# A two-layer attention and mixture kernel on one core: the eight experts of layer 0 get only the tokens routed to them, in 15 blocks of 128 slots

## The chip, the core and the metric

One core of a Trainium2 chip runs the whole program. The metric is device time in microseconds of that core; lower is better. Five engines work side by side, each in its own program order: TensorE (PE), VectorE (DVE), ScalarE (ACT), GpSimd (POOL), and SyncE (SP), which here only issues transfers. They meet through semaphores.

## What is computed

The input is 8 sequences (called batches below) of 512 tokens with 128 numbers each. Layer 0 adds a latent attention (16 heads of 8) and a mixture of experts to the input. Layer 1 adds a mix of three attentions and a gated feed-forward of width 512. The part that the change touches is the mixture:

```
logits = jnp.einsum('bsd,de->bse', x, Wg) + bg
_, top_idx = jax.lax.top_k(logits, K)          # K = 2 of E = 8
sel = jnp.sum(jax.nn.one_hot(top_idx, E, dtype=logits.dtype), axis=-2) > 0
masked = jnp.where(sel, logits, -jnp.inf)
gates = jax.nn.softmax(masked, axis=-1)
for e in range(E):
    h = jax.nn.relu(jnp.einsum('bsd,dh->bsh', x, W1[e]) + b1[e])     # 128 -> 512
    y = jnp.einsum('bsh,hd->bsd', h, W2[e]) + b2[e]                  # 512 -> 128
    out = out + gates[..., e:e + 1] * y
```

Each token has two experts with a gate above zero. The two four-head attentions of layer 1, called `ca` and `mc` here, are the other part: `softmax(q k) v` with 512 keys per sequence.

## The kernel before

**Time grid.** A table `AT` gives every piece of work of a batch a step number G, and each engine walks through the steps in order and does what is due in it. Batch b is shifted by `S = 80` steps, so that in steady state three batches overlap and every 80 steps the pattern repeats. Work at step 112 of one batch stands beside step 32 of the next; below, "step" is the number modulo 80, from 0 to 79, and a "cycle" is 80 such steps. Each step holds one attention unit (two heads of one chunk of 128 queries): PE makes two score tiles, DVE takes their row maxima (L725 for the causal groups `a0`, L729 for the others), 15 steps later PE makes the transposed scores, ACT takes the exponentials into `probs`, and every second step PE multiplies by the values. Steps 0 to 31 hold the units of `a0`, 32 to 39 `ca`, 40 to 63 and 72 to 79 `a1`, 64 to 71 `mc`. PE may not write a score tile before DVE has reduced the tile two before it (semaphore `max`), so PE and DVE stay within about a step of each other. No engine passes by a waiting instruction.

**Experts.** `up(b, i)` (32 per batch, steps 7 to 40) makes 128 of an expert's hidden rows for all 512 tokens: three float16 passes (high and low halves of weights and tokens) of 512 columns into bank U. ACT reads the bank twice, for `hm` (L1060) and `h_hi` (L1061), and POOL subtracts for `h_lo` (L1162). `down(b, e, c)` (32 per batch, steps 15 to 45) is 12 matmuls of 128 columns into bank N. DVE adds each expert's output times its gate to `xs` (L829, 4 per expert, steps 17 to 45). All experts run on all tokens; the gates of the others are zero. All weights lie in SBUF as `w_hi` and `w_lo` from the start.

**Gates.** `rank_parts` compares all pairs of logits (L764 to L775, steps 78 and 79), and `gate_weights` follows at step 6.

**Key sums.** In `ca` and `mc`, `value(g, c)` multiplies the exponentials of chunk c with the values (4 float32 matmuls, `probs,vc`) and then with ones (4 more, `probs,ones`) for the softmax denominators: four chunks for each of the 16 groups.

**Feed-forward and others.** `fa`, `fb`, `glu`, `g1`, `g2`, `f3` of the batch before run at steps 51 to 79 and 0 to 11; DVE scales each of their banks (L882, L887, L892), POOL makes low halves (`glu_low`, L1203). POOL also sums the rotary parts (L1182 and `halves`, steps 50 and 65), masks the causal tiles (L1150) and takes square roots (L1169). SP issues the transfers that spread q and k over partitions (`relq`, `relk`) and the row maxima (`mrow`).

## Time and profile before

| | us |
|---|---|
| median of three runs | 1853.18 (1851.37 to 1859.51) |
| the profiled execution | 1848.13 |
| its span, first to last instruction | 1846.4 |
| PE busy in the span | 1654.0 (90%) |
| DVE / ACT / POOL busy | 1206.7 / 1171.5 / 690.3 |
| data moved by transfers | 66.82 MB |

The page of the profile has the busy times, 40 slices of the span, the transfer queues, the chain of work that ended last, the groups of instructions and the transfers. A busy PE time is a union of instructions whose ends include the drain of the array; the distance between two starts tells what a matmul costs in a stream. The stages of a cycle are read by windows of time: the pairs of DVE's row maxima were counted, two per step, to find where the steps of batch 4 begin.

### The profile page before, as it was taken

What the parts mean: (1) busy time and instruction counts of PE and PEld (TensorE: products, weight loads), DVE (VectorE), ACT (ScalarE), POOL (GpSimd) and SP (SyncE); (2) the same over time, 40 slices, a digit from 0 to 9 for tenths busy, and PEclk for the clock granted to TensorE, in tenths of its full rate; (3) what the DMA queues carried; (4) which work ended last, traced back from release to release, by engine and by line L of the source; (5) the groups of instructions that cost most, each with busy time, mean ns of one, the idle gap of its engine ahead of it and who ended that gap; (6) DMA issues with size and microseconds to landing.
All of it is one profiled execution on the core that took longest, in us unless ns stands there. A gap on an engine that the chain in (4) does not pass through costs nothing.

```text
span 1846.4 us, 33580 instructions
## 1 busy us (share of the span) xinstructions
PE 1654.0 (90%) x12402; PEld 707.3 (38%) x12402; DVE 1206.7 (65%) x3101; ACT 1171.5 (63%) x2226; POOL 690.3 (37%) x672
## 2 busy tenths in 40 slices
PE   3886899889999999999999999999999999988876
PEld 1343453245333543345333543345333543322231
DVE  6545478556876588666876588666876568476633
ACT  2681766577656875687657865687666865635442
POOL 3453652255232652255232652255232641211120
PEclk9996999999999999999999999999999999989986
DMA  5101100101101101101101101101100100010010
GB/s 212 35 19 35 59 19 16 55 13 30 47 23 36 42 25 41 47 19 30 47 24 36 42 24 46 41 18 31 45 30 31 36 24 24 31 39 18 18 35 6
DMA packets 63683, 66.82 MB, mean 36 GB/s; under 512 B 8144, under 2 KB 58144, under 8 KB 62624
## 3 DMA queue, kind: packets, MB, share of 16 engines
q1 hardware_dynamic: 63520, 64.68, 11.4%
q8 instruction: 99, 1.62, 0.4%
q14 instruction: 64, 0.52, 0.1%
HBM read 40.73 MB, written 23.59 MB: 35 GB/s over the span
## 4 chain that ended last, share of the span: by engine, by line
PE 71%; DVE 12%; ACT 10%; issue 5%; DMA 1%; POOL 1%; SPq 1%; POOLq 0%; ACTq 0%; DVEq 0%
PE banks L366 69%; DVE negmax L729 5%; ACT probs L1000 3%; ACT h_hi L1061 2%; DVE h L892 2%; ACT hm L1060 2%; ACT L1000 1%; DVE r_b L917 1%; ACT h L1095 1%; DVE h L887 1%; PE banks L586 1%; DVE xs L829 1%; ACT L1095 0%; DVE g_t L882 0%; DVE mrow L736 0%
## 5 line engine op out<-in xcount | busy, mean ns | idle before, releaser
L1000 ACT ACTIVATE probs<-banks 128x512 f32<-128x512 f32 (+3 forms) x1280 | 614.3, 535 | 442.8 <-PE banks L366 438.6
L729 DVE TENSOR_REDUCE negmax<-banks 128x1 f16<-128x512 f32 x768 | 493.0, 685 | 149.7 <-PE banks L366 146.6
L1162 POOL TENSOR_TENSOR h_lo<-hm,h_hi 128x512 f16<-128x512 f32 x256 | 296.6, 1159 | 383.2 <-ACT h_hi L1061 383.1
L725 DVE CUSTOM_DVE_ANT_0 scr<-banks,mask_row 128x384 f32<-128x384 f32 (+3 forms) x512 | 230.3, 487 | 212.0 <-PE banks L366 210.2
L366 PE MATMUL banks<-kp,qs 32*128 32x512 f16 (+3 forms) x1024 | 236.0, 361 | 46.6 <-DMA kp<-relk 22.4
L1060 ACT ACTIVATE hm<-banks,cols 128x512 f32<-128x512 f32 x256 | 177.3, 693 | 105.7 <-PE banks L366 104.5
L366 PE MATMUL banks<-probs,vp 128*32 128x512 f32 (+3 forms) x2048 | 241.8, 545 | 0.0
L366 PE MATMUL banks<-qs,kp 32*128 32x512 f16 (+3 forms) x1024 | 199.5, 355 | 35.6 <-ACT probs L1000 32.6
L1203 POOL TENSOR_TENSOR h_lo<-h,h_hi 128x512 f16<-128x512 f32 x96 | 110.3, 1169 | 290.1 <-ACT h_hi L1089 212.4
L366 PE MATMUL banks<-w_hi,h_hi 128*128 128x128 f16 x1152 | 204.0, 220 | 0.0
L366 PE MATMUL banks<-w_lo,h_hi 128*128 128x128 f16 x1152 | 203.6, 220 | 0.0
L366 PE MATMUL banks<-w_hi,h_lo 128*128 128x128 f16 x1152 | 203.5, 220 | 0.0
L366 PE MATMUL banks<-qkc 97*128 97x512 f16 (+1 forms) x512 | 166.6, 400 | 12.2 <-DMA qkc<-mrow 4.3
L1061 ACT ACTIVATE h_hi<-banks,cols 128x512 f16<-128x512 f32 x256 | 176.2, 688 | 0.0
L366 PE MATMUL banks<-xh,w_hi 128*128 128x512 f16 x320 | 127.5, 399 | 49.4 <-ACT h_hi L1061 30.7
L366 PEld LDWEIGHTS banks<-kp,qs 32*128 32x128 f16 x1024 | 63.4, 92 | 264.8 <-issue 101.8
L366 PE MATMUL banks<-xl,w_hi 128*128 128x512 f16 x320 | 124.4, 389 | 0.0
L366 PEld LDWEIGHTS banks<-w_hi,h_hi 128*128 128x128 f16 x1152 | 113.2, 98 | 29.2 <-issue 11.7
L366 PE MATMUL banks<-xh,w_lo 128*128 128x512 f16 x320 | 124.3, 389 | 0.0
L366 PEld LDWEIGHTS banks<-w_lo,h_hi 128*128 128x128 f16 x1152 | 113.2, 98 | 18.1 <-issue 0.7
L366 PEld LDWEIGHTS banks<-w_hi,h_lo 128*128 128x128 f16 x1152 | 113.2, 98 | 0.0
L1154 POOL TENSOR_TENSOR halves<-w,halves 128x512 f16<-128x512 f32 x64 | 74.5, 1164 | 98.5 <-ACT halves L1020 96.6
(163 smaller groups left out, 2377.2 us busy)
## 6 DMA issues: line engine op xcount, KB each, us to landing
qkc<-relm SPq DMA_DIRECT2D x96, 128.0 KB, 2.9
qs<-relq SPq DMA_DIRECT2D x64, 128.0 KB, 2.1
kp<-relk SPq DMA_DIRECT2D x64, 128.0 KB, 2.2
relm<-halves SPq DMA_DIRECT2D x32, 256.0 KB, 2.1
relq<-halves SPq DMA_DIRECT2D x16, 256.0 KB, 2.1
relk<-halves SPq DMA_DIRECT2D x16, 256.0 KB, 2.1
h<-split_in SPq DMA_DIRECT2D x3, 1024.0 KB, 5.2
xs<-x_in SPq DMA_DIRECT2D x8, 256.0 KB, 2.8
```

The lines of the kernel that those rows point to most:

```text
L366: return nc.tensor.matmul(psum[rows_, bank, cols_], lhsT, rhs, start=start, stop=stop)
L586: last = nc.tensor.transpose(psum[:, M, ch(c)], osb[:, g.main % 2, ch(c)], C("ident"))
L725: v.tensor_tensor_reduce(scr[:, s, 0:kw], psum[:, SCO + s, 0:kw], mask_row[:, T - kw:T], -1.0, 3e38, ALU.add, ALU.min, negmax[:, g.n % 2, ...
L729: v.tensor_reduce(negmax[:, g.n % 2, c, h:h + 1], psum[:, SCO + s, 0:kw], AX.X, ALU.max, negate=True).then_inc(sem("max"), 1)
L829: ins = v.scalar_tensor_tensor(out=xs[:, b % 4, c, :], in0=psum[:, N, ch(c)], scalar=gates[:, c, e:e + 1], in1=xs[:, b % 4, c, :], op0=ALU ...
L892: v.tensor_scalar(h32[:, o, :], psum[:, U, :], V(f"hs{n}", o), None, ALU.mult) \
L1000: a.activation(probs[:, c % 2, 2 * pair + s, q0:T], psum[:, TRA + s, q0:T], ACT.Exp, scale=SCALE[main(g)]).then_inc(sem("exp"), 1)
L1060: a.activation(hm[:, i % 2, :], psum[:, U, :], ACT.Relu, bias=V("b1", i))
L1061: a.activation(h_hi[:, (e + 1) % 2, hc, :], psum[:, U, :], ACT.Relu, bias=V("b1", i)) \
L1154: p_.tensor_tensor(out=halves[:, w, 1, :], in0=w32[:, w, :], in1=halves[:, w, 0, :], op=ALU.subtract).then_inc(sem(f"low{w}"), 1)
L1162: p_.tensor_tensor(out=h_lo[:, (e + 1) % 2, hc, :], in0=hm[:, i % 2, :], in1=h_hi[:, (e + 1) % 2, hc, :], op=ALU.subtract).then_inc(sem("h ...
L1203: p_.tensor_tensor(out=h_lo[:, k % 2, o, :], in0=h32[:, o, :], in1=h_hi[:, k % 2, o, :], op=ALU.subtract).then_inc(sem("g_lo"), 1)
```

## The change

- **Routing.** `rank_parts` moves from steps 78 and 79 to 45, 46 and 47 of the same cycle, the one before the batch's own, and `gate_weights` from step 6 of its own cycle to 51 of the one before. PE then counts, for every token and expert, the chosen tokens before it (`positions`, 8 small matmuls, step 51), and DVE turns the counts into two slot numbers per token and into the owner expert of each of `NT = 15` blocks of 128 slots (`slots`, 14 operations, step 52; `pick`, 5 operations, step 53). A block belongs to one expert. 1024 routed tokens in blocks of one expert never need more than 15 blocks, and all 15 are always computed.
- **Scatter and gather.** ACT and POOL make high and low halves of the normalised tokens (`xr`), and POOL issues 8 indirect transfers that write them to slots in HBM (`xslots`, steps 53 to 56). SP loads the slots back (`xg_load`), PE turns them (8 transposes per four blocks), ACT copies them out. After the experts, ACT copies the block outputs (`y_out`), SP stores them (`yslots`), POOL issues 8 indirect transfers that gather each token's two rows (steps 44 to 50), and DVE adds them with their gates (8 operations, step 53).
- **Experts.** `up(b, t)` is 12 matmuls of 128 columns for a block (every second step from 10 to 38), ACT makes `hm` in 4 operations of 128 columns, DVE copies its high half (`hh`), POOL makes the low half (`hl`), and `down(b, t)` is 12 matmuls of 128 columns (every second step from 13 to 41).
- **Weights.** At the start the split expert weights are written to HBM (`wexp1`, `wexp2`, 4 MB). For each block SP reads the owner from SBUF into a register, twice, and loads 264 KB and 256 KB (`wup`, `wdn`; 30 loads per batch, three buffers each).
- **Key sums.** In `ca` and `mc` POOL adds the exponentials of chunks 1 and 2 into those of chunk 0 (`psums`, 4 additions of 1024 numbers per partition, steps 50 to 53 and 2 to 5), and PE multiplies `probs` (chunk 3) and `psums` with ones at the last chunk only. ACT waits for the addition before it writes over `probs`.
- Some other pieces move by one or two steps. `scr` becomes bfloat16, and several buffers share space.

```diff
-AT.update({("up", i): at for i, at in enumerate((
...
+AT.update({("up", t): 10 + 2 * t for t in range(NT)})
+AT.update({("down", t): 13 + 2 * t for t in range(NT)})
+AT.update({("wup", t): 6 + 2 * t for t in range(NT)})
+AT.update({("wdn", t): 8 + 2 * t for t in range(NT)})
+AT.update({("scatter", c): at for c, at in enumerate((-27, -26, -25, -24), 0)})
+AT.update({("gather", c): at for c, at in enumerate((44, 46, 48, 50), 0)})
+AT.update({("xg_load", q): at for q, at in enumerate((-22, -21, 8, 16), 0)})
...
-                    three(U, slice(0, T), [(part(w_hi, "W1", i, P), part(w_lo, "W1", i, P), xh[:, 0, :], xl[:, 0, :])]) \
...
+                def up(b, t):
...
+                    pe.wait_ge(sem(f"wup{n % 3}"), 16 * (n // 3 + 1))
+                    own("u", ("up", t), b)
+                    w = wt1[:, n % 3, 0:512].bitcast(F16)
+                    for hc in range(HC):
+                        last = three(U, ch(hc), [(w[:, P * hc:P * hc + P], w[:, 512 + P * hc:512 + P * hc + P],
+                                                  xt[:, q % 2, t % 4, 0, :], xt[:, q % 2, t % 4, 1, :])])
...
-                    if not main(g):
-                        last.then_inc(sem("pv_mix"), 1)
-                        for h in range(GH):
-                            last = mm(N, slice(q0, T), ones[:, :], probs[:, c % 2, h, q0:T], c == 0, c == NC - 1,
-                                      rows_=slice(32 * h, 32 * h + 32))
                     last.then_inc(sem("pv"), 1)
+                    if not main(g) and c == NC - 1:
+                        pe.wait_ge(sem("psums"), 4 * (g.mix + 1))
+                        own("n", "den", g.n)
+                        for part_ in (keys(g, c), psums):
+                            for h in range(GH):
+                                last = mm(N, slice(0, T), ones[:, :], part_[:, h, :], part_ is not psums, part_ is psums,
...
+                            v.tensor_copy(hh[:, n % 2, :], hm[:, n % 2, :]).then_inc(sem("hh"), 1)
+                    if (b := due(G, "add")) is not None:
+                        dve.wait_ge(sem("gath"), 128 * (b + 1))
...
-                            a.activation(hm[:, i % 2, :], psum[:, U, :], ACT.Relu, bias=V("b1", i))
-                            a.activation(h_hi[:, (e + 1) % 2, hc, :], psum[:, U, :], ACT.Relu, bias=V("b1", i)) \
+                            for hc in range(HC):
+                                ins = a.activation(hm[:, n % 2, ch(hc)], psum[:, U, ch(hc)], ACT.Relu, bias=bias[:, hc:hc + 1])
...
+                            for k in range(2):
+                                p_.indirect_dma_start(xslots, bass.IndirectOffsetOnAxis(idx[:, NC * k + c:NC * k + c + 1], 0),
+                                                      xr[:, c, :, :].rearrange("p a d -> p (a d)"), None).then_inc(sem("scat"), 16)
...
+                                p_.indirect_dma_start(yg[:, NC * k + c, :], None, yslots,
+                                                      bass.IndirectOffsetOnAxis(idx[:, NC * k + c:NC * k + c + 1], 0)).then_inc(sem("gath"), 16)
...
+                    p_.tensor_tensor(out=psums[:, hs, :], in0=psums[:, hs, :], in1=probs[:, c % 2, hs, :],
+                                     op=ALU.add).then_inc(sem("psums"), 1)
...
+                    e = sp.value_load(owner[0:1, t:t + 1], min_val=0, max_val=E - 1)
+                    sp.dma_start(wt1[:, n % 3, :], wexp1[bass.ds(e, 1), :, :].rearrange("e p f -> (e p) f")).then_inc(sem(f"wup{n % 3}"), 16)
```

On PE, in the expert stage of a middle batch (`xh`, `xl` tokens, `w_hi`, `w_lo` weights, `kp,qs` and `qs,kp` attention tiles), the kernel before has this:

```order
L366 MATMUL banks<-kp,qs 128x512 x2
L366 MATMUL banks<-qs,kp 128x512 x2
L366 MATMUL banks<-probs,vp 32x512 x4
L366 MATMUL banks<-xh,w_hi 128x512
L366 MATMUL banks<-xl,w_hi 128x512
L366 MATMUL banks<-xh,w_lo 128x512
L366 MATMUL banks<-oc,wide 128x512
L366 MATMUL banks<-kp,qs 128x512 x2
L366 MATMUL banks<-qs,kp 128x512 x2
L366 MATMUL banks<-xh,w_hi 128x512
L366 MATMUL banks<-xl,w_hi 128x512
L366 MATMUL banks<-xh,w_lo 128x512
```

And the changed kernel, at the same place (`xt` turned tokens, `wt` loaded weights, `xg` slots):

```order
L434 MATMUL banks<-kp,qs 128x512 x2
L434 MATMUL banks<-qs,kp 128x512 x2
L434 MATMUL banks<-probs,vp 32x512 x4
L434 MATMUL banks<-xt,wt 128x128 x12
L434 MATMUL banks<-oc,wide 128x512
L434 MATMUL banks<-kp,qs 128x512 x2
L434 MATMUL banks<-qs,kp 128x512 x2
L635 MATMUL banks<-ident,xg 128x128 x8
```

Three matmuls of 512 columns in every step have become twelve of 128 in every second one, with the transposes of slots between.

On DVE, at steps 51 to 54 of a middle batch, the kernel before has row maxima, the heads of layer 0 and the gated feed-forward:

```order
L729 TENSOR_REDUCE negmax<-banks 128x1 x4
L842 RECIPROCAL rden<-banks 128x4x4
L843 TENSOR_TENSOR onorm<-banks,rden 128x4x32
L729 TENSOR_REDUCE negmax<-banks 128x1 x2
L882 SCALAR_TENSOR_TENSOR g_t<-g_t,banks 128x512
L729 TENSOR_REDUCE negmax<-banks 128x1 x2
```

The changed kernel has this between the end of the same heads (step 52) and the same feed-forward operation (step 54):

```order
L898 TENSOR_TENSOR first<-first,off 128x32
L899 TENSOR_TENSOR first<-first,off 128x32
L900 TENSOR_TENSOR late_f<-const,till 1x128
L902 TENSOR_REDUCE best<-first 128x4
L903 TENSOR_REDUCE best<-first 128x4
L906 CAST idx<-best 128x8
L907 TENSOR_REDUCE cnt<-late_f 1x16
L910 TENSOR_SCALAR owner<-cnt 1x16
L825 TENSOR_REDUCE negmax<-banks 128x1 x2
L984 SCALAR_TENSOR_TENSOR xs<-yg,gk,xs 128x128 x8
L915 TENSOR_TENSOR first<-first,best 128x32 x2
L919 TENSOR_TENSOR first<-first,gates 128x32 x2
```

Six more operations of `slots` stand ahead of these and one of `pick` behind. So 14 new operations stand in step 52 and 13 in step 53, with only one pair of row maxima between them.

On POOL, at steps 49 to 57 of a middle batch, before:

```order
L1154 TENSOR_TENSOR halves<-w,halves 128x512 x2
L1182 TENSOR_TENSOR w<-r_a,r_b 128x512
L1184 CAST halves<-w 128x512
L1154 TENSOR_TENSOR halves<-w,halves 128x512
L1203 TENSOR_TENSOR h_lo<-h,h_hi 128x512 x3
L1221 TENSOR_TENSOR oc<-oc,r_b 128x512
```

And in the changed kernel (`psums` are the key sums, the DMA rows the indirect transfers):

```order
L1379 TENSOR_TENSOR psums<-psums,probs 128x1024
L1368 DMA yg<-yslots,idx 128x128 x2
L1398 TENSOR_TENSOR w<-r_a,r_b 128x512
L1400 CAST halves<-w 128x512
L1335 TENSOR_TENSOR halves<-w,halves 128x512
L1379 TENSOR_TENSOR psums<-psums,probs 128x1024 x3
L1353 DMA xslots<-xr,idx 1920x256 x8
L1419 TENSOR_TENSOR h_lo<-h,h_hi 128x512 x3
L1437 TENSOR_TENSOR oc<-oc,r_b 128x512
```

Four additions and ten transfers now stand around the rotary sum and ahead of the feed-forward's low halves.

## Rows read from the trace of the kernel before

**Rows 1.** The page: span, and busy time of each engine.

```profile
span 1846.4 us, 33580 instructions
PE 1654.0 (90%) x12402; PEld 707.3 (38%) x12402; DVE 1206.7 (65%) x3101; ACT 1171.5 (63%) x2226; POOL 690.3 (37%) x672
```

**Rows 2.** The page: chain that ended last, share by engine.

```profile
PE 71%; DVE 12%; ACT 10%; issue 5%; DMA 1%; POOL 1%; SPq 1%; POOLq 0%; ACTq 0%; DVEq 0%
```

**Rows 3.** Windows, batch 4: steps 0-6, 7-31, 32-45, 46-63, 64-79; busy by engine.

```profile
771.05:789.81 18.76, 18.73 (x123) 6.47 (x122) 9.32 (x37) 11.50 (x21) 1.13 (x1) 1.00 0.06 21
789.81:852.82 63.01, 58.90 (x591) 31.70 (x591) 38.30 (x138) 51.87 (x102) 38.41 (x37) 1.00 0.12 31
852.82:887.69 34.87, 34.28 (x349) 18.80 (x348) 28.23 (x74) 24.61 (x59) 19.07 (x20) 1.00 0.07 17
887.69:934.56 46.87, 43.78 (x262) 15.53 (x260) 38.39 (x75) 27.95 (x53) 11.91 (x11) 0.96 0.14 43
934.56:978.62 44.06, 41.25 (x236) 13.99 (x236) 32.71 (x65) 28.08 (x47) 14.41 (x15) 0.96 0.15 49
```

**Rows 4.** Timeline of PE: start, us, form; an `up`, then 24 matmuls of `down`.

```profile
642.45 0.39 PE L366 MATMUL banks<-xh,w_hi 128*128 128x512 f16 x1
...
643.11 0.22 PE L366 MATMUL banks<-w_hi,h_hi 128*128 128x128 f16 x1
...
644.39 0.22 PE L366 MATMUL banks<-w_hi,h_lo 128*128 128x128 f16 x1
```

**Rows 5.** Timeline of PE: a key sum and what follows it.

```profile
700.97 1.04 PE L366 MATMUL banks<-probs,ones 128*32 128x512 f32 x8
701.94 0.39 PE L366 MATMUL banks<-xh,w_hi 128*128 128x512 f16 x1
```

**Rows 6.** Groups of instructions with shapes apart: count, busy us, mean ns, idle before.

```profile
L366 PE MATMUL banks<-probs,ones 128*32 128x512 f32 x512 | 70.4, 623 | 0.0
...
L1060 ACT ACTIVATE hm<-banks,cols 128x512 f32<-128x512 f32 x256 | 177.3, 693 | 105.7 <-PE banks L366 104.5
L1061 ACT ACTIVATE h_hi<-banks,cols 128x512 f16<-128x512 f32 x256 | 176.2, 688 | 0.0
L1000 ACT ACTIVATE probs<-banks 128x128 f32<-128x128 f32 x128 | 28.5, 280 | 29.9 <-PE banks L366 29.9
```

**Rows 7.** The same of DVE: additions of experts, high halves, a two-input operation.

```profile
L829 DVE SCALAR_TENSOR_TENSOR xs<-banks,gates,xs 128x128 f32<-128x128 f32 x256 | 71.8, 343 | 29.4 <-PE banks L366 29.4
...
L900 DVE CAST h_hi<-h 128x512 f16<-128x512 f32 x64 | 28.2, 494 | 0.0
...
L770 DVE TENSOR_TENSOR r_a<-r_a,r_b 128x256 f32<-128x256 f32 x8 | 8.4, 1052 | 0.3
```

**Rows 8.** Timeline of DVE: rank operations at 163 to 167 us.

```profile
165.38 0.43 DVE L770 TENSOR_TENSOR r_a<-r_a,r_b 128x256 f32<-128x256 f32 x1
...
166.38 0.18 DVE L774 TENSOR_REDUCE gmax<-lg 128x4 f32<-128x32 f32 x1
166.60 0.19 DVE L775 TENSOR_TENSOR lg<-lg,gmax 128x32 f32<-128x32 f32 x1
```

**Rows 9.** The same of POOL: low halves.

```profile
L1162 POOL TENSOR_TENSOR h_lo<-hm,h_hi 128x512 f16<-128x512 f32 x256 | 296.6, 1159 | 383.2 <-ACT h_hi L1061 383.1
```

**Rows 10.** Timeline of all engines in the first 40 us.

```profile
20.19 1.27 POOL L1182 TENSOR_TENSOR w<-r_a,r_b 128x512 f32<-128x512 f32 x1 [4.68 <-DVE r_b L756]
...
25.93 5.55 DVE L982 TENSOR_TENSOR w_lo<-probs,w_hi 128x2048 f16<-128x2048 f32 x2
26.09 3.24 POOL L1182 TENSOR_TENSOR w<-r_a,r_b 128x512 f32<-128x512 f32 x1 [2.72 <-DVE r_b L756]
...
38.01 0.43 SPq L1272 DMA_DIRECT2D kp<-relk  x1
38.36 0.29 PE L366 MATMUL banks<-kp,qs 32*128 32x128 f16 x2 [13.07 <-DMA kp<-relk]
```

**Rows 11.** Window: batch 0 from its first steps to the end of its experts.

```profile
43.00:148.00 105.00, 88.97 (x783) 45.23 (x783) 54.54 (x191) 72.42 (x147) 51.28 (x51) 1.00 0.08 24
```

**Rows 12.** The page: transfers; KB each, median us from issue to landing.

```profile
xs<-x_in SPq DMA_DIRECT2D x8, 256.0 KB, 2.8
```

More of the change, by code:

```diff
@@ L170, in first_time @@
 def first_time(name, b):
-    return min(time((*name, c), b) for c in range(NC)) if name[0] == "down" else time(name, b)
+    return time(("down", 4 * name[1]), b) if name[0] == "y" else time(name, b)
 def numbered(names, more=()):
@@ L238, in build @@
         LOWS[name, b] = lows[w]
+    OLD, last = {}, {}
+    for g in GROUPS:
+        for c in range(NC):
+            k = c % 2 if main_kind(g.kind) or c else 2
+            OLD[g.n, c] = last.get(k)
+            last[k] = (g, c)
     CAUSAL = {g.n: n for n, g in enumerate(g for g in GROUPS if g.kind == "a0")}
@@ L458, in value @@
                             taken(pe, "m", "cav" if g.kind == "ca" else "mcv", g.b)
-                            own("n", "den", g.n)
                     _, q0 = width(g, c)
```

478 lines of the change are left out of this document (356 added, 122 removed), and 8 rows, old and new, of the table AT.

## The prediction

> **What bounds the kernel now.** I read the page's busy times first, then the chain, then windows of one cycle in the middle. PE is busy 1654.0 of 1846.4 us [rows 1], and 71% of the chain that ended last runs through it [rows 2]. The average hides that the stages of a cycle differ [rows 3]. In steps 7 to 31 PE is busy 58.9 of 63.0 us, with ACT behind it at 51.9. In steps 32 to 45 it is 34.3 of 34.9, with DVE at 28.2. In steps 46 to 63 PE has 43.8 of 46.9 and DVE already 38.4. In steps 64 to 79 it is 41.3 and 32.7 of 44.1. So PE sets the pace everywhere, but in the last two stages DVE follows closely. PE can't leave DVE behind by more than a step, because of the row maxima. What matters is therefore which engine is busiest in each stage after the change.
>
> **Part 1, expert matmuls.** The three passes of an `up` take 643.11 - 642.45 = 0.66 us; 24 matmuls of 128 columns have 1.28 us from the first start to the last, 0.056 each, so twelve take 0.67 [rows 4]. Before: 32 x 0.66 + 32 x 0.67 = 42.6 us per batch. After: 15 ups and 15 downs of twelve, 20.1, and 30 transposes of 128 columns at 0.056, 1.7, and 8 small matmuls, at most 0.4: 22.2. PE saves 20.4 us per batch. (15 blocks are always computed, so the work falls to about half, not to 2 in 8.)
>
> **Part 2, key sums.** One chunk's sum costs 701.94 - 700.97 = 0.97 us [rows 5]; 512 matmuls in the group, 8 to a chunk, are 8 chunks per batch [rows 6]. Four stay: 3.9 us saved. On PE alone that is (20.4 + 3.9) x 8 = 194 us, a span of 1652. That is the floor, not the forecast.
>
> **Part 3, the stages one by one.** Steady cycle, starting from the windows [rows 3].
> - Steps 7 to 31. PE loses 23 ups and 19 downs (27.9), gets 11 ups and 10 downs (14.1), transposes (1.7) and one key sum more (1.0): 58.9 becomes 47.8. ACT loses 23 pairs of readings at 0.69 each, 31.7, and gets 44 operations of 128 columns at 0.28 (12.3) and copies of about 7 at 0.69 per 512 columns [rows 6]: 39. DVE loses 16 additions of 0.343 and gets 11 copies of 0.49 [rows 7]: 38. POOL loses 23 low halves of 1.16 and gets 11 [rows 9]. PE still leads. With the gap of before, 4.1, the window is 52: -11.0.
> - Steps 32 to 45. PE loses 9 ups and 13 downs (14.6) and gets 9 pieces of 0.67: 25.7. DVE: 28.2 - 5.5 + 4 x 0.49 + 0.9 for the first rank operations = 25.6. Two engines that wait for each other at equal load leave more gaps than one: 29.5, -5.4.
> - Steps 0 to 6. Three of four key sums of `mc` leave: -2.6.
> - Steps 46 to 63. Here the change works against itself. DVE gets the rest of the rank work (2.9), gate weights (4 x 0.22), `slots` (14 x 0.22 = 3.1), `pick` (5 x 0.22 = 1.1) and 8 additions at 0.343 (2.7). The 0.22 is the distance of two linked small operations [rows 8]. Sum 10.6, so DVE has 49.0, PE 43.8 - 1.9 + 0.4 = 42.3: DVE is now the bound, and the 27 operations in steps 52 and 53 come as one lump, which PE can't run past. With the gap of before (3.1) the window is 52.1: +5.2.
> - Port waits in that stage. When DVE and POOL both work on SBUF they delay each other: a rotary sum took 1.27 us alone and 3.24 beside two large DVE subtractions [rows 10], and a two-input DVE operation took 0.43 alone [rows 8] and 1.05 on average [rows 7]. POOL is now full in steps 50 to 56: four additions of 1024, at twice 1.16 = 2.3 us each [rows 9], and three rotary pieces. Each can hold up one DVE operation: between 0 and 9.3 + 3.1 = 12.4 us. I take 4, about seven meetings at the 0.6 us that the row shows. Stage in all: +9.2.
> - The Trainium skill ("SBUF — State Buffer", SBUF: two separate sides) calls the port pair that the two share an exclusive lock for a whole instruction, and warns that a POOL-issued transfer can't get its descriptors written while DVE holds it. The slowed rows agree with the lock; by the full rule the stage would carry the whole 12.4 us and the span would be 50 us longer.
> - Steps 64 to 79. The rank work has left; PE is the bound: -1.
>
> Sum over the cycles: seven batches in steady state x (-16.4) = -115; seven times -2.6 = -18; six cycles x (+9.2) = +55, and +1.5 in the seventh; six x (-1) = -6. Together -82.
>
> **Part 4, the start and batch 0.** PE's first score waits for the k transfer until 38.4 us, and that chain runs through a rotary sum on POOL [rows 10]. Ahead of it now stand the rank work and `slots` on DVE (about 5 us) and 8 indirect transfers on POOL: +12. Batch 0 runs its experts with little beside them: 105 us, PE 89.0 [rows 11]. The 20.4 us of PE come off nearly whole: -20. After its last block nothing covers the way back: `y_out` 0.7, store 2.8 [rows 12], 8 gathers, landing 2.8, additions 2.7, less the additions of before: +14. A last key sum or two: -2. Together +4.
>
> **Part 5, transfers and what hides them.** Block loads are 30 x 260 KB per batch, 62 MB more beside 66.8 MB. A transfer of 256 KB lands in 2.8 us [rows 12], and each load is issued four steps ahead, of about 2.1 us each. Hidden. On SP a load needs an issue of 0.43 us [rows 10] and a register read. No row shows the read: between 0.43 (an issue) and 2.8 (a transfer's round trip). Two loads must fit into two steps, 4.2 us, so up to 1.7 us a read is free. I take 1. An indirect transfer on POOL isn't in the trace either: between 0.43 (an issue) and 2.8 (a round trip), below nothing excluded since POOL issued none. I take 1.0, nearest to POOL's own operations of 1.16 [rows 9]. In a steady cycle it is covered: from step 50 POOL has 10 transfers, 9.3 us of additions, 3.1 of rotary pieces and a low half, 24 us, and the first that PE misses is the low half at step 62, 12 steps or 35 us later. The Trainium skill ("DMA: Bandwidth & Descriptors", Anatomy of one DMA — SWDGE (gpsimd) path) gives about 2.0 us fixed for such a transfer, mostly until its completion is confirmed; if POOL were held for it, an estimate from that page is +18 us at the start and at batch 0's end, and the steady cycles would just hold.
>
> **The sum.** 1846.4 - 82 + 4 = 1768 us of span. The profiled run's own time is 1.7 above its span, and the median of the runs shown 5.1 above that: 1775.
>
> **Rivals.**
> - *PE alone counts.* The new DVE work fits into gaps, and the port waits don't come. For it: PE leads in all five windows. Against: 49.0 us of DVE can't fit into 46.9 [rows 3]. 1652 plus the start's 26 gives 1678, as a median 1685. Chance 0.17.
> - *The gain is lost in steps 46 to 63.* Port waits at their upper bound, 8.4 x 6 = +50, and PE's granted clock falling to 1.2 GHz in longer gaps, as it did to a mean of 0.96 in this window: 1825 to 1860. Chance 0.17.
> - *Slower: POOL's indirect transfers.* Ten stand ahead of the low halves. With T us each the free 35 us are used up at T = 2.1; at T = 3.2 the gain of 78 us is gone; at T = 4 it is 19 us per cycle, +133 and the start's longer waits: about 1910. Also behind them: SP at step 58 waits for the scatter and holds back the row maxima of the next group. Chance 0.13.
> - *Slower: SP's register reads.* At 2.8 us a block needs 6.5 us against 4.2: 34 us per batch, about 1970 after the gain. It decides from 2.0 us a read, where 10 us per batch are lost. Chance 0.05.
> - My forecast, 1715 to 1825: chance 0.48.
>
> **How the numbers follow.** The likeliest case gives 1775. Below 1665 nothing reaches but mistakes in the floor; above 1870 lies most of the two slower rivals. The range is 1665 to 1870. A measurement here can tell about 0.5% from no change, 1844 to 1862. Faster: 0.48 + 0.17 + most of the second rival, 0.75. Same: 0.06. Slower: 0.19.
>
> **What would show it.** In the profile after: PE busy near 1480 us; steps 7 to 31 at 50 to 54 us with PE waiting little; steps 46 to 63 at 52 to 57 us, longer than now, with PE waiting for DVE's maxima at the lump and DVE's two-input operations above their lone durations; first score near 50 us. Wrong if PE waits for `wt` loads, if POOL's low halves come late to `g1`, or if the stage 46 to 63 hasn't grown.

## The result: slower by 2.7%

The changed kernel takes 1905.5 us (median of 4 runs, 1898.5 to 1909.1), the kernel before, run beside it, 1854.5 (1851.4 to 1859.5). The ratio is 1.0268, with a 95% interval of 1.0230 to 1.0306. I had forecast 1775 in a range of 1665 to 1870, so the sign is wrong too. Run 5 and v2 below each had one execution in a much slower state (3282 and 2461 us); these are in no median or ratio here, and v2's stages are read from its second run. The page of the changed kernel, lines that answer to [rows 1, 2]:

```profile
span 1904.7 us, 34002 instructions
PE 1548.5 (81%) x11490; PEld 658.2 (35%) x11490; DVE 1290.5 (68%) x3199; ACT 1038.7 (55%) x2258; POOL 812.5 (43%) x728
PEclk9985887999899998999899998999898998979876
PE 52%; DVE 19%; issue 10%; ACT 9%; POOL 4%; DMA 3%; SPq 3%; POOLq 0%; ACTq 0%; DVEq 0%
```

TensorE has 105 us less to do and is idle 164 us more. Its share of the chain that ended last went from 71 to 52%. The five windows of batch 4, as in [rows 3] (steps 0 to 6, 7 to 31, 32 to 45, 46 to 63, 64 to 79; the columns are length, then busy time and number of instructions of each engine, granted clock, DMA share, GB/s):

```profile
804.16:820.81 16.65, 16.62 (x100) 5.75 (x99) 8.65 (x32) 11.04 (x20) 10.41 (x5) 1.00 0.16 48
820.81:882.84 62.03, 52.13 (x584) 29.62 (x584) 38.94 (x132) 42.63 (x112) 26.25 (x26) 0.97 0.51 141
882.84:914.22 31.38, 28.15 (x270) 15.14 (x273) 26.08 (x65) 18.64 (x53) 12.23 (x14) 0.94 0.30 91
914.22:974.20 59.98, 46.40 (x262) 15.63 (x263) 54.41 (x117) 27.13 (x53) 37.14 (x31) 0.84 0.20 60
974.20:1019.33 45.13, 41.31 (x227) 13.57 (x227) 31.00 (x54) 28.22 (x47) 14.40 (x14) 0.92 0.14 45
```

Set against the forecast (us; the last column is version v2, below, in its second run):

| steps | before | forecast | changed | v2 |
|---|---|---|---|---|
| 0 to 6 | 18.8 | 16.2 | 16.7 | 19.2 |
| 7 to 31 | 63.0 | 52.0 | 62.0 | 54.9 |
| 32 to 45 | 34.9 | 29.5 | 31.4 | 30.1 |
| 46 to 63 | 46.9 | 56.1 | 60.0 | 47.6 |
| 64 to 79 | 44.1 | 43.1 | 45.1 | 45.4 |
| cycle | 207.6 | 196.8 | 215.2 | 197.3 |

A cycle is 18.4 us over the forecast, 10.0 of them in steps 7 to 31. The start came as forecast: the first score is at 48.7 us, 10 later than before. Over the whole run, in us against the kernel before: start +10.3, batch 0 (its steps 0 to 79) +1.2, batches 1 and 2 +14.5, batches 3 to 6 +7.6 each, the rest +1.8.

**What stands in the lump.** VectorE's timeline of step 52 (start, us, engine, line, operation, tiles) shows the slot arithmetic:

```profile
932.97 0.17 DVE L897 TENSOR_TENSOR till<-till,begin 128x8 f32<-128x8 f32 x1
933.17 1.15 DVE L898 TENSOR_TENSOR first<-first,off 128x32 f32<-128x32 f32 x1
934.25 0.18 DVE L899 TENSOR_TENSOR first<-first,off 128x32 f32<-128x32 f32 x1
934.46 2.31 DVE L900 TENSOR_TENSOR late_f<-const,till 1x128 f32<-1x128 f32 x1
936.70 0.17 DVE L902 TENSOR_REDUCE best<-first 128x4 f32<-128x32 f32 x1
936.99 2.01 DVE L906 CAST idx<-best 128x8 uint32<-128x8 f32 x1
938.91 0.27 DVE L907 TENSOR_REDUCE cnt<-late_f 1x16 f32<-1x128 f32 x1
939.22 2.08 DVE L910 TENSOR_SCALAR owner<-cnt 1x16 int32<-1x16 f32 x1
```

GpSimd at the same time (the third line is the second of the three additions by itself), and after it TensorE's next score, with what it waited for in brackets:

```profile
933.13 1.15 POOL L1335 TENSOR_TENSOR halves<-w,halves 128x512 f16<-128x512 f32 x1
934.24 7.03 POOL L1379 TENSOR_TENSOR psums<-psums,probs 128x1024 f32<-128x1024 f32 x3
936.59 2.38 POOL L1379 TENSOR_TENSOR psums<-psums,probs 128x1024 f32<-128x1024 f32 x1
941.95 1.20 PE L434 MATMUL banks<-kp,qs 32*128 32x512 f16 x2 [9.78 <-DVE negmax L825]
```

The three additions take 2.33 to 2.39 us and end at 936.63, 938.97 and 941.27. L900, L906 and L910 end at 936.77, 939.00 and 941.30, each just behind one of them, and L898 ends at 934.32, behind L1335 at 934.28. An operation on sixteen numbers took 2.08 us. The reductions between them took 0.16 to 0.27, and L899, which starts 0.01 us after the first addition, took 0.18. GpSimd's additions weren't stretched by it (their mean over the run is 2.362).

**What TensorE waited for in all** (total us, times, longest); in the trace of before the first of these groups had 12.6 us in 45 waits:

```profile
PE banks L434 <- DVE negmax L825: 86.0, 79, 9.9
PE banks L434 <- ACT probs L1165: 50.3, 39, 3.0
PE banks L434 <- issue: 39.8, 35, 5.8
```

### The profile page after: what moved, and what is told of

It reads as the page before. It is cut to its first block, busy times and chain, and to the rows that moved or that the text cites. A ratio compares the mean times of both kernels' runs of the same rounds, so it can differ in the third digit from the quotient of the medians.

```text
span 1904.7 us, 34002 instructions
## 1 busy us (share of the span) xinstructions
PE 1548.5 (81%) x11490; PEld 658.2 (35%) x11490; DVE 1290.5 (68%) x3199; ACT 1038.7 (55%) x2258; POOL 812.5 (43%) x728
## 4 chain that ended last, share of the span: by engine, by line
PE 52%; DVE 19%; issue 10%; ACT 9%; POOL 4%; DMA 3%; SPq 3%; POOLq 0%; ACTq 0%; DVEq 0%
PE banks L434 50%; DVE negmax L825 7%; ACT probs L1165 3%; ACT hm L1234 3%; DVE h L1049 1%; DMA qkc<-relm 1%; SPq L1509 1%; DVE pack L832 1%; DVE r_b L1074 1%; ACT L1165 1%; POOL xslots L1353 1%; DVE xs L984 1%; DVE xn L846 1%; POOL yg L1368 1%; ACT h L1276 1%
## 5 line engine op out<-in xcount | busy, mean ns | idle before, releaser
L821 DVE CUSTOM_DVE_ANT_0 scr<-banks,mask_row 128x384 bf16<-128x384 f32 (+3 forms) x512 | 230.1, 487 | 166.7 <-PE banks L434 164.9
L1359 POOL TENSOR_TENSOR hl<-hm,hh 128x512 f16<-128x512 f32 x120 | 139.0, 1158 | 260.3 <-DVE hh L979 260.2
L1379 POOL TENSOR_TENSOR psums<-psums,probs 128x1024 f32<-128x1024 f32 x64 | 149.7, 2362 | 128.1 <-PE banks L434 128.1
L1234 ACT ACTIVATE hm<-banks,wt 128x128 f32<-128x128 f32 x480 | 137.6, 370 | 116.7 <-PE banks L434 116.1
L434 PE MATMUL banks<-wt,hh 128*128 128x128 f16 x960 | 96.3, 223 | 34.3 <-issue 29.4
L434 PE MATMUL banks<-xt,wt 128*128 128x128 f16 x1440 | 107.0, 227 | 6.0 <-issue 5.8
L434 PE MATMUL banks<-h_hi,w_hi 128*128 128x512 f16 x256 | 98.9, 386 | 9.6 <-DVE h L1049 8.8
L434 PEld LDWEIGHTS banks<-xt,wt 128*128 128x128 f16 x1440 | 86.6, 102 | 52.6 <-issue 48.6
L1335 POOL TENSOR_TENSOR halves<-w,halves 128x512 f16<-128x512 f32 x64 | 74.1, 1158 | 57.4 <-ACT halves L1185 55.1
L434 PE MATMUL banks<-h_hi,w_lo 128*128 128x512 f16 x256 | 97.8, 382 | 0.0
L434 PE MATMUL banks<-h_lo,w_hi 128*128 128x512 f16 x256 | 97.7, 382 | 0.0
```

Of the source, the lines that this page charges most:

```text
L434: return nc.tensor.matmul(psum[rows_, bank, cols_], lhsT, rhs, start=start, stop=stop)
L821: v.tensor_tensor_reduce(scr[:, s, 0:kw], psum[:, SCO + s, 0:kw], mask_row[:, T - kw:T], -1.0, 3e38, ALU.add, ALU.min, negmax[:, g.n % 2, ...
L1234: ins = a.activation(hm[:, n % 2, ch(hc)], psum[:, U, ch(hc)], ACT.Relu, bias=bias[:, hc:hc + 1])
L1335: p_.tensor_tensor(out=halves[:, w, 1, :], in0=w32[:, w, :], in1=halves[:, w, 0, :], op=ALU.subtract).then_inc(sem(f"low{w}"), 1)
L1359: p_.tensor_tensor(out=hl[:, n % 2, :], in0=hm[:, n % 2, :], in1=hh[:, n % 2, :], op=ALU.subtract).then_inc(sem("h_lo"), 1)
L1379: p_.tensor_tensor(out=psums[:, hs, :], in0=psums[:, hs, :], in1=probs[:, c % 2, hs, :], op=ALU.add).then_inc(sem("psums"), 1)
```

## The experiments

Each time is a median; the ratio is to the kernel before, run beside it on the same chip; the changed kernel itself stands at 1.0268 (1.0230 to 1.0306). "Theory A" is the lump behind GpSimd's additions.

**1. Additions made small.**

```
-  out=psums[:, hs, :], in0=psums[:, hs, :], in1=probs[:, c % 2, hs, :]
+  out=psums[:, hs, 0:1], in0=psums[:, hs, 0:1], in1=probs[:, c % 2, hs, 0:1]
```

> The changed kernel, except that each of GpSimd's 64 key sum additions takes one column of 512 per head and so leaves the sums incomplete; every wait and every other instruction stays. Theory A (the lump of slot arithmetic on VectorE in step 52 is slow because each of several of its small operations stands behind a whole 2.3 us addition of GpSimd): step 52 falls from 11.8 us to about 4, the operations at L900, L906 and L910 from 1.6 to 1.8 us to about 0.2, PE's wait of 9.8 us before the next score is nearly gone, and with the clock that is kept the run takes 65 to 90 us less than the changed kernel's 1905: 1815 to 1840. Theory B (these operations are slow by themselves: one partition, conversions to integers): they stay at 1.5 us and more, step 52 stays above 9 us, and the time stays within 20 us of 1905. Theory C (TensorE's lower clock is a cause of its own and not a result of its gaps): the gap goes, the mean granted clock stays near 0.90 and at most half of the gain comes.

Measured 1858.6 us, 1.0044 (1.0019 to 1.0069): 2.2% or 41 us less than the changed kernel. The same operations on VectorE, at the same place:

```profile
924.73 0.28 DVE L900 TENSOR_TENSOR late_f<-const,till 1x128 f32<-1x128 f32 x1
925.23 0.17 DVE L906 CAST idx<-best 128x8 uint32<-128x8 f32 x1
925.61 0.16 DVE L910 TENSOR_SCALAR owner<-cnt 1x16 int32<-1x16 f32 x1
```

Their own cost is 0.16 to 0.28 us and the whole arithmetic takes 2.7 us, so theory B falls. TensorE's wait before the next score is 2.4 us, and step 52 falls from 11.8 to 4.4 us. Steps 46 to 63 are at 55.8 us in the mean of batches 3 to 6, against 60.8 in the changed kernel and 45.7 before. Theory A is right, but for 41 us, not 65 to 90: the additions account for 5.0 of that stage's growth of 15.1 us. Part of what step 52 gives is lost one step earlier, where a small operation of the gate weights (0.19 us in the changed kernel) now meets a rotary sum of GpSimd and ends just behind it:

```profile
920.03 1.39 DVE L928 TENSOR_TENSOR gates<-gates,gsum 128x32 f32<-128x32 f32 x1
920.08 1.28 POOL L1398 TENSOR_TENSOR w<-r_a,r_b 128x512 f32<-128x512 f32 x1
```

Where the stage grew can be read step by step (means of batches 3 to 6, changed kernel less before): steps 46 and 47, where the rank work now stands, 3.0 us, step 52 9.0, step 53 with the additions to `xs` and `pick` 3.2. The signs of theory C came too: the granted clock is 0.90 to 0.91 over the run and 0.86 in this stage (0.84 in the changed kernel), though TensorE's wait shrank from 9.8 to 2.4 us, and about half of the expected gain came. So this run shows what the additions cost, but not whether the lower clock is only a result of the gap.

**2. The key sums alone.** The kernel before, with `value`, `exp_unit` and the new `sum_keys` as in the changed kernel; to make room, small tensors share storage and `scr` is bfloat16, as there.

> The kernel before with only the key sums moved to GpSimd as in the changed kernel (its dense experts stay). To make room, small tensors share storage and the masked scores' scratch is bf16, as in the changed kernel. TensorE has 3.9 us per batch less. Theory A (the additions hurt only because the slot arithmetic meets them): few VectorE operations of the kind that stand behind them are in steps 50 to 53, so the time is 1820 to 1850, 5 to 30 us under before. Rival (GpSimd's additions hold up VectorE's casts and sums, and ScalarE's buffers, wherever they stand): 1860 to 1890, with VectorE's negated maxima coming late in steps 50 to 53 and 2 to 5.

Measured 1848.5 us, 0.9982 (0.9957 to 1.0008). Part 2 by itself is worth nothing or next to it. Steps 46 to 63 stay at 45.9 us, so the additions don't lengthen it there, with two key sums (1.9 us by [rows 5]) taken off TensorE; but steps 7 to 31 go from 63.9 to 67.1 (means of batches 3 to 6), and that takes back the 2.6 us of steps 0 to 6. The price of the additions in the changed kernel comes from meeting the slot arithmetic.

**3. The slot arithmetic 17 steps later, gate weights, `pick` and scatters 17 to 20, the additions left where they are.**

```
-"gates": -29, "pos": -29, "slots": -28, "pick": -27, ... scatter (-27, -26, -25, -24), xg_load (-22, -21, ...)
+"gates":  -9, "pos": -11, "slots": -11, "pick": -10, ... scatter (-10, -9, -8, -7),    xg_load (-3, -2, ...)
```

In this kernel `pick` ran one step ahead of the gate weights, so the picked values weren't the final weights; all instructions are there.

> The changed kernel with the positions, slot arithmetic, gate weights, pick and scatters moved 18 steps later (positions and slots from steps 51 and 52 to 69, gate weights to 71, pick to 70, scatters to 70 to 73, the first slot loads to 77 and 78), where GpSimd does no additions and VectorE has room; the work is all there. Theory A: step 52 falls to about 3.5 us, the lump of some 4 us in steps 69 to 71 mostly fits beside TensorE's work (VectorE was busy 6.5 of 10.7 us there), and the run is 50 to 80 us under the changed kernel: 1825 to 1855; the start is also up to 8 us shorter, since 8 scatters no longer stand ahead of the k transfer. Theory B (the operations are slow by themselves): the lump of 10 us moves along, steps 69 to 71 get 5 us or more longer, and the time is 1890 to 1915.

Measured 1953.4 us, 1.0548 (1.0505 to 1.0592): 50 us slower than the changed kernel, where theory A in my reading wanted it 50 to 80 faster. Steps 64 to 79 grow from 45.4 to 56.0 us, steps 46 to 63 shrink only from 60.8 to 59.5 (means of batches 3 to 6). The by-form groups of VectorE (busy, mean ns), and TensorE and GpSimd at steps 71 and 72:

```profile
L984 DVE SCALAR_TENSOR_TENSOR xs<-yg,gk,xs 128x128 f32<-128x128 f32 x64 | 65.9, 1089 | 9.4 <-DMA yg<-yslots,idx 9.1
L900 DVE TENSOR_TENSOR late_f<-const,till 1x128 f32<-1x128 f32 x8 | 2.2, 280 | 0.3
1014.86 1.08 POOL L1353 DMA_INDIRECT xslots<-xr,idx  x1 [12.27 <-DVE idx L906]
1021.31 0.96 POOL L1353 DMA_INDIRECT xslots<-xr,idx  x1 [0.30 <-issue]
1022.29 1.16 POOL L1391 TENSOR_TENSOR xl<-wide,xh 128x512 f16<-128x512 f32 x1
1023.51 0.61 PE L434 MATMUL banks<-xh,l_hi 128*128 128x512 f16 x1 [6.52 <-POOL xl L1391]
```

Two things. The slot arithmetic is cheap once no addition is beside it (0.28). But the eight additions to `xs`, next in the queue, now stand behind GpSimd's key sums in its place (mean 1089 ns, 421 in the changed kernel), and step 53 takes 11.8 us as step 52 did. And the six scatters seen there, 0.96 us of GpSimd each and 0.30 between two, hold back the low half `xl` that TensorE needs. My fear of transfers on GpSimd was a real mechanism; it was harmless only where the change had put them.

**4. No register reads.** `e = t // 2` in place of both `value_load`, so each block gets a fixed expert's weights.

> The changed kernel with every block's weights loaded from a fixed expert (block number divided by two) instead of the one read from the owner table; sizes, number and waits of the transfers stay, and the results are those of the wrong experts. This takes the 30 register reads a batch off SyncE's queue. My forecast's term (reads of up to 1.7 us are free): within 5 us of 1905. Rival (loads and the transfers queued behind them come late because of the reads, which the trace puts at about 0.8 us each, and cause part of TensorE's waits in steps 7 to 45): 1875 to 1895, with the wait for the qkc transfer at step 31 (1.2 to 1.5 us) gone.

Measured 1909.7 us, 1.0306 (1.0254 to 1.0358): no gain. The reads are free, as forecast.

**5. Downs one step later.**

```
-("down", t): 13 + 2 * t;  y_out (20, 28, 36, 42);  y_store (21, 29, 37, 43);  "ca_spread": 110
+("down", t): 14 + 2 * t;  y_out (21, 29, 37, 42);  y_store (22, 30, 38, 43);  "ca_spread": 109
```

> The changed kernel with each block's second matmul one step later (14 + 2t in place of 13 + 2t), the copies of the first three result banks one step later too, and the mixing transfer of step 30 back at 29 as before the change. Theory D (the gain of steps 7 to 31 went into TensorE's waits for hand-offs: a down that opens a new bank waits for ScalarE's copy y_out, which stands behind four ReLU pieces of the same step, and the first down for POOL's low half; measured gaps of 0.9 to 1.8 us at steps 13, 21, 29, 31 and 37): about 5 to 6 us per batch come back, steps 7 to 45 fall from 93 to 88, the run to 1855 to 1875. Theory E (ScalarE, VectorE and GpSimd are paced by the four-step chain itself, and a wait removed turns up at the next step): within 10 us of 1905.

Measured 1974.7 us, 1.067 (1.061 to 1.073), 69 us slower than the changed kernel. TensorE's waits just ahead of the downs did go (in steps 7 to 45 of batch 4 from 4.1 us in four waits to none over 0.15), but a down and the up two blocks on now stand in the same even step, and the odd steps have neither; the waits for row maxima grew from 86.0 to 102.6 and those of the masked groups from 15.1 to 37.5 us. From step 14 to 41 the even steps take 45.4 us in all in place of 33.9, the odd ones 24.0 in place of 28.9 (means of batches 3 to 6). So how evenly TensorE's work lies over the steps counts, which no busy time shows.

**6. TensorE kept busy through the gap.** `back0`'s four transposes 17 times.

> The changed kernel, in which TensorE repeats the four transposes of back0 (step 53) 17 times over in batches 0 to 6, the same result into the same bank, about 9 us of work in place of the 10 us in which it waited there for VectorE's lump. Theory C (the lower clock that follows the gap is a cost of its own): the granted clock in steps 54 to 63 stays at 1.0, where the trace of the changed kernel counts 4 to 6 us per batch of matmul time added by the half clock in steps 46 to 63, and the run is 15 to 35 us shorter: 1870 to 1890. Rival (those steps are set by VectorE, busy 40.6 of 44.7 us, and the clock only uses up slack): within 8 us of 1905, or longer by what the repeats overrun.

Measured 1910.3 us, 1.031 (1.0265 to 1.0356): no gain. The clock of steps 46 to 63 rose only from 0.84 to 0.86 in batch 4, and the repeats made the stage longer (63.0 us against 60.8, means of batches 3 to 6), so this doesn't decide what the clock costs; it stays open.

**7. One ReLU per block.** The biases of three of the four chunks are left out.

```
-for hc in range(HC): a.activation(hm[:, n % 2, ch(hc)], ..., bias=bias[:, hc:hc + 1])
+a.activation(hm[:, n % 2, :], psum[:, U, :], ACT.Relu, bias=bias[:, 0:1])
```

> The changed kernel with one ReLU of 512 columns per block in place of four of 128 (1.15 us by the trace of the changed kernel, against 0.69 for one of 512 before the change). All four chunks of hidden units get the first chunk's bias, so the other biases are left out. ScalarE loses 15 x 0.46 = 7 us per batch, and the bank that up, xg and ReLU share comes free 0.46 us earlier. Theory D (hand-offs pace steps 7 to 45): 3 to 6 us per batch less, 1865 to 1885. My forecast (TensorE's own work paces them, ScalarE has room at 61 of 93 us): within 8 us of 1905.

Measured 1884.7 us, 1.0165 (1.0116 to 1.0215): 20 us less. ScalarE, with 61 us of work in the 93 of steps 7 to 45, is far from full, and still 7 us per batch taken off it bring something: steps 7 to 31 fall by 2.3 us in the mean of batches 3 to 6. But steps 32 to 63 give 3.2 us back there, at a lower granted clock (0.89 for 0.96 in steps 32 to 45, 0.81 for 0.84 in 46 to 63), and these cycles are 0.9 us longer in all. The 20 us come from batch 0 (7.4), batch 1 (9.6) and the time after batch 6 (7.4). So the run speaks for hand-offs in steps 7 to 31, but doesn't price them over a steady cycle.

**8 and 9. Two thirds of the expert matmuls taken away**, from the changed kernel and from the one before (only the high halves are multiplied).

> The changed kernel with one pass instead of three in each block's up and down (only the high halves are multiplied, the two corrections are left out). Everything else stays, the low halves on GpSimd too. TensorE has 30 x 8 x 0.056 = 13.5 us per batch less, all but a little of it in steps 7 to 45. Forecast's premise (TensorE's own work sets the pace of steps 7 to 45): steps 7 to 45 fall from 92.5 to about 80 and the run by 90 to 105 us, to about 1805. Theory F (with the dense experts gone these steps are paced by hand-offs from TensorE to ScalarE or VectorE and back, step by step, and TensorE's work only fills them): less than half of it comes back, 20 to 45 us, 1860 to 1885.

> The kernel before with one pass instead of three in each of its 32 ups and 32 downs (the two corrections are left out), so TensorE has 64 x 0.44 = 28.5 us per batch less, in steps 7 to 45, which is a little more than the change takes off there; nothing else is touched, no routing, no loads. Forecast's premise: steps 7 to 45 fall from 98.8 to about 75, the run by 180 to 220 us, to about 1650. Theory F (a floor under these steps from the chain of hand-offs and from ScalarE's 76 us): they fall to 85 to 90, and the run by 70 to 110 us, to 1745 to 1785.

The first measured 1916.1 us, 1.0363 (1.0303 to 1.0423), the second 1789.4, 0.9676 (0.9624 to 0.9728). Windows of batch 4, steps 7 to 31 and 32 to 45, of the first and then of the second:

```profile
829.54:891.38 61.84, 53.03 (x416) 24.48 (x416) 38.88 (x132) 42.77 (x112) 25.82 (x26) 0.75 0.53 144
891.38:925.41 34.03, 30.03 (x198) 13.08 (x201) 25.90 (x65) 18.67 (x53) 13.93 (x17) 0.75 0.27 81
```

```profile
755.70:813.55 57.85, 48.67 (x393) 21.69 (x393) 38.36 (x137) 50.87 (x102) 38.44 (x37) 0.88 0.13 33
813.55:848.91 35.36, 30.51 (x227) 13.06 (x227) 29.40 (x74) 24.48 (x60) 19.01 (x21) 0.85 0.06 16
```

168 matmuls fewer in steps 7 to 31 of the changed kernel, and the stage stays at 61.8 us (62.0 before the edit); TensorE's busy time in it doesn't fall either (53.0 against 52.1). In the kernel before, 28.5 us of TensorE's work per batch, more than the change takes off, bring 61 us in 8 batches: 0.27 us for each microsecond. Steps 32 to 45 don't get shorter at all (35.4 against 34.9). Behind it are two candidates that these runs don't part: the steps may not be able to follow each other faster than scores, maxima and exponentials allow (argued, not shown), and the granted clock falls when the work goes (0.97 to 0.75, and 1.00 to 0.88), so that what is left takes longer.

**10. Shorter additions.** Each of 1024 columns as two of 512.

> The changed kernel with each of GpSimd's key sum additions of 1024 columns (2.36 us) split into two of 512, the same work and sums. Theory A as a lock (a VectorE operation of the affected kind waits until GpSimd's whole instruction has ended): L900, L906 and L910 fall from 1.6 to 1.8 us to about half, 0.7 to 1.1 us, the adds' own total stays, step 52 falls from 11.8 to 8 or 9 us, and the run by 10 to 25 us. Rival (the two share a bandwidth, so VectorE's operations are slowed in proportion and the length of GpSimd's instruction doesn't matter): their means and step 52 stay within 10%, the run within 6 us of 1905.

Measured 1898.2 us, 1.0306 (1.0214 to 1.0398), too wide to tell the run from the changed kernel. The operations tell the theories apart (the mean in the changed kernel was 1800, 1548 and 1599 ns):

```profile
L900 DVE TENSOR_TENSOR late_f<-const,till 1x128 f32<-1x128 f32 x8 | 8.0, 999 | 0.3
L906 DVE CAST idx<-best 128x8 uint32<-128x8 f32 x8 | 5.9, 740 | 0.3
L910 DVE TENSOR_SCALAR owner<-cnt 1x16 int32<-1x16 f32 x8 | 6.3, 790 | 0.3
```

Half the length of GpSimd's instruction, half the wait: VectorE waits for its end. In batch 4 step 52 fell from 11.8 to 8.7 us, but step 53 rose from 5.0 to 7.0, since the rest of the additions then met the adds to `xs` (mean 588 ns in place of 421).

**11 to 16. Putting the parts back in better order.** v1 has the key sums on TensorE as before the change, positions and slots in step 69, gate weights in 68, scatters in 78 to 81, and the later downs of run 5; e13 is the same with the downs back at 13 + 2t; e11 and e12 are the changed kernel with one small move each; v2 is e13 with both moves.

> A version built from what the first runs showed: routed blocks as in the changed kernel, but all key sums on TensorE as before the change; positions and slot arithmetic in step 69, gate weights in 68, pick in step 1, scatters in steps 78 to 1, the first slot loads in steps 4 and 5, downs and bank copies placed as in the run with the later downs. Theory A (the lump was slow by the additions beside it, and costs only where VectorE is near its limit): steps 46 to 63 near 50 us in place of 60, steps 64 to 79 at 45 to 47, steps 7 to 45 at 88 to 90, a cycle of 203 to 206, and with the start 5 us shorter 1820 to 1855, at or below before. Rival (every placement of the lump and of eight scatters costs about what it gives): 1875 to 1900.

> The version v1 with each down back at 13 + 2t, so that ups stand in even and downs in odd steps, the copies of the result banks at steps 20, 28 and 36 again but ahead of the ReLUs of their step in ScalarE's queue, and the mixing transfer at step 27. Theory: v1's cycle of 212.4 had 64.3 and 34.5 us in steps 7 to 31 and 32 to 45, where the changed kernel has 61.6 and 30.9, since both matmuls of a block in one step leave the other step idle; with these back and the waits at the result bank shorter, a cycle of 203 to 207 and a run of 1825 to 1855, at or under before. Rival (the gain of the dropped waits turns up as another wait, as in the run with the later downs): 1870 to 1890.

> The changed kernel with the four copies of result banks (y_out, same steps) ahead of that step's ReLUs in ScalarE's program order, nothing else. Theory D (steps 7 to 45 are paced by who waits in which queue; the first down on a new bank stood 1.1 to 1.8 us behind y_out, and y_out behind 1.15 us of ReLU): 2 to 3.5 us per batch, 1880 to 1890. Rival (the wait turns up elsewhere, as with the later downs): 1900 to 1910.

> The changed kernel with the six transfers of ca_spread at step 27 in place of 30, nothing else. TensorE waited 1.3 to 1.5 us for them before the first score of the mixing group (step 31). Theory D: that wait goes, about 10 us in all, 1893 to 1898. Rival: they now stand ahead of two weight loads on SyncE's queue (6 x 0.45 = 2.7 us), which come late, 1905 or more.

> The version v2 without its two small steps (copies back behind the ReLUs, ca_spread at 30), so the changed kernel with key sums on TensorE and with slot arithmetic, pick and scatters moved away from step 52. If the parts add up, v1 at 1901 less the 72 us that the later downs cost gives about 1830, with steps 46 to 63 near 49 us in place of 61 (12 us per cycle, 80 in all) and steps 7 to 45 unchanged at 92 to 93. Rival (v2's gain is mostly in its two small steps): 1860 to 1890.

> The version v2 a second time, for a trace in which its stages can be read (the first one was taken at half clock from the middle on). Expected 1770 to 1785. From the parts: steps 46 to 63 at 48 to 50 us, steps 7 to 31 at 57 to 59 and 32 to 45 at 29 to 30, first score near 38 us.

| kernel | us | ratio to before | interval |
|---|---|---|---|
| changed | 1905.5 | 1.0268 | 1.0230 to 1.0306 |
| v1 | 1901.3 | 1.0263 | 1.0218 to 1.0308 |
| e11, bank copy ahead of ReLUs | 1874.2 | 1.0135 | 1.0088 to 1.0182 |
| e12, mixing transfer earlier | 1889.0 | 1.0226 | 1.0181 to 1.0270 |
| e13, sums and slots | 1816.9 | 0.9831 | 0.9788 to 0.9873 |
| v2 | 1777.0 | 0.9615 | 0.9563 to 0.9668 |
| v2 again | 1782.9 | 0.9632 | 0.9607 to 0.9656 |

The edit of e11, in ScalarE's `experts`, moves four lines:

```
+  for q in range(NC): if due(G, ("y_out", q)): ... a.activation(yv, psum[N]) -> n_taken
   for t in range(NT):  if due(G, ("up", t)):    ... four ReLUs -> u_taken
-  for q in range(NC): if due(G, ("y_out", q)): ... a.activation(yv, psum[N]) -> n_taken
```

What it cures stands in the trace of the changed kernel at step 21:

```profile
856.30 1.15 ACT L1234 ACTIVATE hm<-banks,wt 128x128 f32<-128x128 f32 x4 [1.17 <-PE banks L434]
857.32 0.61 ACT L1241 ACTIVATE yv<-banks 128x512 f32<-128x512 f32 x1
858.03 0.27 PE L434 MATMUL banks<-wt,hh 128*128 128x128 f16 x2 [1.50 <-issue]
```

The down opens a new result bank, which has to be copied out first; the copy stands behind four ReLUs of the next block, and those behind TensorE. "issue" means that the profile shows no releaser; the copy's end at 857.93, 0.10 us before the down, is it, and in e11's trace three of the four waits ahead of downs are gone (4.1 us to 0.8 in steps 7 to 45 of batch 4). By the ratios e11 gives 1.3%, e12 0.4% (its interval overlaps that of the changed kernel, so it is not shown by itself; its trace lacks the wait of 1.4 us for `relm` before the first mixing score of batch 4), e13 4.4%. Together 6.1%, and v2 has 6.4: the parts add up. e13 itself moves the key sums and the slot work at once; by run 1 the additions are 2.2 of its 4.4%, and no run parts the rest. v2, windows of batch 4 and TensorE's waits:

```profile
747.29:766.51 19.22, 19.19 (x124) 6.52 (x123) 9.46 (x37) 11.88 (x21) 4.78 (x5) 1.00 0.32 97
766.51:821.40 54.89, 49.64 (x576) 29.18 (x576) 38.78 (x132) 41.50 (x111) 25.76 (x26) 1.00 0.60 164
821.40:851.51 30.11, 27.61 (x270) 14.26 (x273) 25.89 (x65) 18.65 (x54) 13.03 (x16) 0.96 0.31 87
851.51:899.15 47.64, 43.98 (x270) 15.52 (x266) 43.12 (x93) 27.21 (x53) 19.42 (x19) 0.99 0.20 54
PE banks L434 <- ACT probs L1158: 45.3, 41, 2.8
PE banks L434 <- DVE negmax L823: 28.5, 75, 1.1
PE banks L434 <- issue: 8.8, 8, 4.3
```

With the lump gone steps 46 to 63 are nearly where they were before the change (47.6 us against 46.9 in batch 4, 49.2 against 45.7 in the mean of batches 3 to 6), the longest wait for the maximum of an unmasked group is 1.1 us in place of 9.9, and that stage's clock is 0.99 in batch 4, and 0.96 in the mean, in place of 0.84. v1 shows by its 1901 that run 5's loss is real: e13 differs from it by the downs and their bank copies, and by one step of the mixing transfer, and is 84 us faster.

## Why the prediction was wrong

- **Part 1, the work of the expert matmuls: right, but not in busy time.** TensorE lost 105.5 us of busy time, not the 194 of parts 1 and 2. Most of the difference can be the clock. Spells at 1.2 GHz make up 174 us of the kernel before (mean granted clock 0.953) and 389 of the changed one (0.898), and TensorE is busy for 137 and 287 us in them. Eight `probs,vc` matmuls take 1.06 us at full clock (929.70 in the changed kernel) and 1.94 in such a spell (944.04); if all matmuls take about twice as long there, an estimate, the spells add 69 us before and 144 after, 75 of the 88 us that are missing.
- **Part 2, key sums: the saving was real, its worth wasn't.** I took off 3.9 us per batch; alone it brings nothing that can be measured (run 2).
- **Part 3, steps 7 to 31: the step that failed first.** I wrote "PE still leads. With the gap of before, 4.1, the window is 52". The gap became 9.9 (62.03 less 52.13), and the busy time 52.1, not 47.8. The premise, "So PE sets the pace everywhere", with matmuls credited at their duration, doesn't hold in runs 8 and 9: matmuls taken away bring nothing in the first and 0.27 us for each microsecond in the second, where steps 32 to 45, with TensorE busy 34.3 of 34.9 us before, get no shorter. The gap isn't a constant that can be carried over, and neither is the clock. How much of this is the tie to the other engines and how much the clock stays open. Of the added waits some have names in the order of the changed program: the down behind the bank copy behind the ReLUs (e11: 61.6 to 59.8 us in steps 7 to 31, means of batches 3 to 6), and the mixing transfer (1.4 us in batch 4). v2's 54.9 comes within 3 us of my 52, so the window was attainable, but not as the change had placed it.
- **Part 3, steps 32 to 45: nearly right,** 31.4 against 29.5.
- **Part 3, steps 46 to 63: right mechanism, mis-sized.** I had the lump in step 52, VectorE as the bound and the port waits, and gave +9.2; batch 4 shows +13.1, the mean of batches 3 to 6 +15.1. The mis-sized terms are the lump and the gap. For `slots` with its port waits I had 14 x 0.22 = 3.1 us and 4: from L888 at 931.15 to the end of L910 at 941.30 it took 10.2, and run 1 puts 41 us of the run on the additions. I had priced the meetings at the 0.6 us of one slowed row, seven of them. They are few but whole: three of 2.0 to 2.3 us, one of 1.15 and one of 0.88 (L891, 0.22 in run 1). And the gap of before, 3.1 us, became 5.6 (59.98 less VectorE's 54.41, where I had 53.0 with the port waits). The rule that I had set aside gives this better. The Trainium skill ("SBUF — State Buffer", SBUF: two separate sides) has the pair of ports locked for a whole instruction, the other engine fully blocked; the ends of L900, L906 and L910 behind the ends of the additions, and run 10, agree.
- **Steps 64 to 79:** I expected -1 and got +1.
- **Part 4:** the start is +10.3 where I had +12; in run 3, where the slot work and the scatters no longer stand ahead of it, the start is +1.0. Batch 0 is +1.2 us over its 80 steps where I had -6 with its way back.
- **Part 5: right.** An indirect transfer takes 0.98 to 1.07 us on GpSimd (I took 1.0; busy, mean ns, idle before). Two loads on SyncE's queue stand 1.17 us apart, with an issue of 0.34, so a read is 0.8 us (I took 1), and none of it shows in the time (run 4). Weight loads land in 2.9 and 2.7 us (I took 2.8). From the changed kernel's groups, its timeline of SyncE and its page:

```profile
L1353 POOL DMA_INDIRECT xslots<-xr,idx x64 | 68.2, 1065 | 21.7 <-issue 18.1 <-DVE idx L906 3.6
L1368 POOL DMA_INDIRECT yg<-yslots,idx x64 | 62.5, 976 | 28.9 <-DMA yslots<-yv 14.7 <-issue 13.5 <-POOL psums L1379 0.2
846.40 0.34 SPq L1545 DMA_DIRECT2D wt<-wexp  x1
847.57 0.34 SPq L1538 DMA_DIRECT2D wt<-wexp  x1
wt<-wexp SPq DMA_DIRECT2D x120, 258.0 KB, 2.9
wt<-wexp SPq DMA_DIRECT2D x120, 256.0 KB, 2.7
```

- **The rivals.** "The gain is lost in steps 46 to 63" came nearest, but it ended at 1860, since it left the 16 us of steps 7 to 45 in place. No rival said that these don't come. The one on GpSimd's transfers has its mechanism in run 3, away from where the change put them.
- **Slips in the sums.** ScalarE's terms for steps 7 to 31 add up to 37.3 us, not 39 (measured 42.6). Less 194, TensorE's busy time would be 1460 us, not 1480. The rival on register reads loses 34 us in each of seven cycles at 2.8 us a read, so it would be at about 2010, not 1970. None of them moves the forecast.

What remains open: whether the lower clock costs anything of its own, and with it what bounds steps 7 to 45. Runs 8 and 9, in which TensorE had less to do, show it lower, run 1 shows it hardly higher with most of the gap gone, and run 6, meant to settle it, hardly raised it.
